# Six of 64 row-maximum reduces of an attention head moved from VectorE to ScalarE and GpSimd

## The reference, cut to what matters

```python
mod = (silu(c) @ wmod).reshape(2, 6, 1, -1)
ga = (2 * (ga >= 0) - 1) * maximum(abs(ga), 0.25)     # a gate, gb likewise
h = layernorm(x) * (1 + ca) + sa
Q, K, V = lora_linear(h, ...)                         # each (2, 2048, 16, 16)
energy = einsum("nqhd,nkhd->nhqk", Q, K) / sqrt(16)
out = einsum("nhqk,nkhd->nqhd", softmax(energy, axis=-1), V)
x = x + ga * lora_linear(out, Wo, bo, Ao, Bo)
h = layernorm(x) * (1 + cb) + sb
x = x + gb * ffn(h)                                   # shared expert + best of 8 experts
```

## Time and profile before

| what | value |
|---|---|
| time, median of 3 runs | 1997.99 us (1996.38 to 2003.76) |
| profiled execution | 2001.02 us, its span 1999.3 us |
| mean granted TensorE clock | 0.978 |
| PE busy | 1883.2 us, 94% |
| VectorE busy | 1576.3 us, 79% |
| ScalarE busy | 1179.2 us, 59% |
| GpSimd busy | 322.2 us, 16% |
| reduces of maxima units | 2048, 1276.8 us busy |

### The profile page before, as it was taken

One profiled execution on the slowest core, in us unless ns is written; L12 is line 12 of the kernel. 1 busy time (PEld: TensorE's weight loads), 2 busy tenths in 40 slices (PEclk: granted clock), 3 DMA queues, 4 the chain that ended last, 5 costly groups with the idle time before them and its releaser, 6 DMA issues.

```text
span 1999.3 us, 33500 instructions
## 1 busy us (share of the span) xinstructions
PE 1883.2 (94%) x12334; PEld 705.1 (35%) x12335; DVE 1576.3 (79%) x2802; ACT 1179.2 (59%) x1354; POOL 322.2 (16%) x361
## 2 busy tenths in 40 slices
PE   7688999999999999999999999999975799999997
PEld 5332222222222222222222222222224555666664
DVE  4377999999999999999999999999816632254443
ACT  4534777777777777777777777777761221111111
POOL 5535000000000000000000000000016532323332
PEclk9898999999999999999999999999997799999999
DMA  4541111211111111111111111111056433222221
GB/s 152 169 148 37 41 41 50 64 44 41 41 60 57 39 41 55 58 46 38 42 60 56 42 38 53 56 43 38 11 171 214 139 106 116 95 78 71 68 66 47
DMA packets 89734, 141.48 MB, mean 71 GB/s; under 512 B 13104, under 2 KB 60208, under 8 KB 89472
## 3 DMA queue, kind: packets, MB, share of 16 engines
q1 hardware_dynamic: 74336, 102.01, 16.2%
q0 software_dynamic: 10240, 32.40, 4.9%
q10 hardware_dynamic: 5024, 5.24, 0.8%
HBM read 90.84 MB, written 48.51 MB: 70 GB/s over the span
## 4 chain that ended last, share of the span: by engine, by line
PE 83%; DVE 4%; issue 4%; POOL 3%; DMA 3%; ACT 1%; SPq 1%; POOLq 0%; DVEq 0%; ACTq 0%
PE ps L853 25%; PE ps L842 21%; PE ps L808 16%; PE ps L1514 7%; PE ps L1065 5%; PE ps L1532 3%; PE ps L1398 3%; DVE mx L909 2%; DMA l_in<-inverse_sums 2%; POOL parts L693 1%; ACT prob L947 1%; POOL rest L689 1%; PE ps L1523 1%; DMA qk_parts<-parts 1%; POOL k_low L681 1%
## 5 line engine op out<-in xcount | busy, mean ns | idle before, releaser
L909 DVE TENSOR_REDUCE mx<-ps 128x1 f32<-128x512 f32 x2048 | 1276.8, 682 | 47.4 <-PE ps L808 42.9
L947 ACT ACTIVATE prob<-ps 128x1024 f32<-128x1024 f32 x1024 | 992.3, 1021 | 294.6 <-PE ps L842 292.3
L853 PE MATMUL ps<-prob,vs 128*32 128x512 f32 x4096 | 546.4, 605 | 0.7 <-ACT prob L947 0.7
L808 PE MATMUL ps<-k_high,q_high 64*128 64x512 bf16 x2048 | 411.9, 388 | 32.4 <-DMA k_low<-qk_parts 17.5
L842 PE MATMUL ps<-q_high,k_high 64*128 64x512 bf16 x2048 | 389.6, 377 | 3.4 <-ACT prob L947 2.5
L842 PE MATMUL ps<-q_low,k_low 34*128 34x512 bf16 x2048 | 389.8, 377 | 0.0
L808 PEld LDWEIGHTS ps<-k_high,q_high 64*128 64x128 bf16 x2048 | 100.9, 92 | 670.6 <-DVE mx L909 603.7
L975 POOL COPY vs<-v_all 128x256 f32 (+1 forms) x32 | 12.7, 400 | 1138.3 <-PE ps L853 1138.2
L842 PEld LDWEIGHTS ps<-q_low,k_low 34*128 34x128 bf16 x2048 | 100.0, 94 | 117.5 <-issue 0.3
L1563 ACT ACTIVATE esig<-ps 128x512 f32<-128x512 f32 x39 | 23.3, 597 | 195.9 <-PE ps L1514 195.9
L842 PEld LDWEIGHTS ps<-q_high,k_high 64*128 64x128 bf16 x2048 | 101.4, 96 | 86.9 <-ACT prob L947 27.9
(11 more groups left out here) (145 smaller groups left out, 1312.4 us busy)
## 6 DMA issues: line engine op xcount, KB each, us to landing
k_high<-qk_parts SPq DMA_DIRECT2D x128, 128.0 KB
qk_parts<-parts SPq DMA_DIRECT2D x32, 384.0 KB, 3.6
q_high<-qk_parts SPq DMA_DIRECT2D x128, 64.0 KB
k_low<-qk_parts SPq DMA_DIRECT2D x128, 64.0 KB
head_out<-head_out_sb SPq DMA_DIRECT2D x32, 256.0 KB, 10.8
sorted_in<-zero_row POOLq DMA_DIRECT2D x13, 390.0 KB, 7.0
xs<-sorted_in SPq DMA_DIRECT2D x39, 130.0 KB
q_low<-qk_parts SPq DMA_DIRECT2D x128, 32.0 KB
```

The costliest lines, as they stand in the source:

```text
L808: pe.matmul(ps[:, ring_bank(2 * m + u), :], q_high[p][mine, t * P:(t + 1) * P], k_high[p][mine, c * CH:(c + 1) * CH], start=True, stop=Tru ...
L853: mm = pe.matmul(ps[32 * j:32 * j + 32, 7, :], vs[buf(h)][:, kt, :], prob[:, kt % 2, j * CH:(j + 1) * CH], start=(kt == 0), stop=(kt == KT ...
L909: dve.tensor_reduce(mx[:, at, c:c + 1], ps[:, ring_bank(k), :], AX.X, ALU.max).then_inc(s_ring, 1)
L947: act.activation(prob[:, kt % 2, :].rearrange("p (u c n) -> p u c n", u=2, c=2)[:, :, half, :], ps[:, 2 * half:2 * half + 2, :], ACT.Exp). ...
```

## The change

**Copied units.** In each head but the first, six pairs (3, 7, 13, 17, 23, 27) have their second unit (u = 1) taken by ScalarE: it copies the bank of 128 x 512 to one of three buffers `taken` behind the exponentials of that iteration, and counts `s_copied`. GpSimd folds the copy to 64 columns in three steps of halving. [...] The six folded units stand in `folded`; one reduce on VectorE turns them into the six columns of `mx`. `mx` and `folded` are doubled.

**Turned maxima.** A table (`Ring`) lists the order of all units and turned maxima, and who frees each bank. The negation is now behind pair 0 of the next head (both units), and the turned maxima behind its third pair (`TURN_AT` = 2).

**Lead.** `LEAD` is 12, so pair 0 falls into iteration 11.

**GpSimd.** The gates are split and stand between the folds of heads 1 and 2; a head's staging and DMA stand behind its second fold. In each head: pair 3, pair 7, staging and DMA, pair 13, 17, 23, 27.

```diff
-LEAD = 10
+LEAD = 12
+TURN_AT = 2
+FOLDS = 3
+FOLDED = 64
+COPIED = (3, 7, 13, 17, 23, 27)
+class Ring:
+    def __init__(self):
+        self.place, self.released = {}, []
+        count = {"dve": 0, "act": 0}
+        for n in range(NH + 1):
+            for m in range(PAIRS if n < NH else 0):
+                for u in range(2):
+                    self.add((n, m, u), "act" if copied(n, m) and u else "dve", count)
+                if n and m == TURN_AT:
+                    self.add((n - 1, "turned"), "dve", count)
+        self.add((NH - 1, "turned"), "dve", count)
...
+        def ring_place(pe, what):
+            at = ring.place[what]
+            if at >= RING:
+                engine, n = ring.released[at - RING]
+                pe.wait_ge(s_ring if engine == "dve" else s_copied, n)
+            return ps[:, ring.bank(what), :]
...
         def max_pair(pe, h, m):
+            banks = [ring_place(pe, (n, m, u)) for u in range(2)]
+            for u in range(2):
...
         def turn_maxima(pe, h):
+            bank = ring_place(pe, (num(h), "turned"))
             pe.wait_ge(s_neg, num(h) + 1)
...
                     if beside:
                         max_pair(pe, who, first)
-                    elif first == 0 and after == 1:
-                        turn_maxima(pe, plus(h, 1))
+                    if first == TURN_AT and num(who) <= NH:
+                        turn_maxima(pe, plus(who, -1))
                     weigh(h, kt - 1)
...
+            def negate(n):
+                if n:
+                    dve.wait_ge(s_fold, n * len(COPIED))
+                    rows = mx[n % 2][:].rearrange("p t c -> p (t c)")[:, UNITS // 2:UNITS // 2 + 30]
+                    dve.tensor_reduce(rows.rearrange("p (i k) -> p i k", k=10)[:, :, 3:8:4], folded[n % 2][:], AX.X,
+                                      ALU.max).then_inc(s_unfold, 1)
+                    dve.wait_ge(s_unfold, n)
+                dve.wait_ge(s_ring, ring.taken((n, PAIRS - 1, 0 if copied(n, PAIRS - 1) else 1)))
+                dve.tensor_reduce(mneg[:], mx[n % 2][:], AX.X, ALU.max, negate=True).then_inc(s_neg, 1)
...
             for n in range(1, NH):
-                head((0, n), last=n == NH - 1)
+                for m in range(PAIRS):
+                    reduce_pair(dve, (0, n), m)
+                    if m == 0:
+                        negate(n - 1)
+                    if m == TURN_AT:
+                        turned_maxima(dve, step, (0, n - 1))
...
+            def take_maxima(n, m):
+                if n >= NH or not copied(n, m):
+                    return
+                k = fold_number(n, m)
+                wait(act, s_fold, k - FOLDS + 1)
+                act.wait_ge(s_max, ring.made((n, m, 1)))
+                act.copy(taken[k % FOLDS][:], ps[:, ring.bank((n, m, 1)), :]).then_inc(s_copied, 1)
...
+            def fold(n, m):
+                k = fold_number(n, m)
+                rows, j = taken[k % FOLDS], COPIED.index(m)
+                pool.wait_ge(s_copied, k + 1)
+                w = CH // 2
+                while w >= FOLDED:
+                    a, b = rows[:, 0:w], rows[:, w:2 * w]
+                    step(pool.tensor_tensor(a, a, b, ALU.subtract))
+                    step(pool.tensor_scalar(a, a, 3.0e38, 0.0, ALU.min, ALU.max))
+                    if w > FOLDED:
+                        step(pool.tensor_tensor(a, a, b, ALU.add))
+                    w //= 2
+                wait(pool, s_unfold, n - 2)
+                pool.tensor_tensor(folded[n % 2][:, j // 2, j % 2, :], a, b, ALU.add).then_inc(s_fold, 1)
...
+            scale_modulation(pool, step)
+            for m in COPIED:
+                fold(1, m)
+                if m == COPIED[1]:
+                    gate(pool, step, 0)
+                if m == COPIED[5]:
+                    gate(pool, step, 3)
+            for n in range(2, NH):
+                for m in COPIED:
+                    fold(n, m)
+                    if n == 2 and m == COPIED[0]:
+                        gate_bias(pool)
+                    if m == COPIED[1] and n + 1 < NH:
+                        following(n)
```

More of the change, by code:

```diff
@@ L112, in close, with add, bank, made @@
         self.count, self.loop = self.first + trips * per, None
+class Ring:
[9 more added lines that the diff above has]
+        self.add((NH - 1, "turned"), "dve", count)
+        self.total = count
+    def add(self, what, engine, count):
+        self.place[what] = len(self.released)
+        count[engine] += 1
+        self.released.append((engine, count[engine]))
+    def bank(self, what):
+        return 4 + self.place[what] % RING
+    def made(self, what):
+        return self.place[what] + 1
+    def taken(self, what):
+        return self.released[self.place[what]][1]
+def copied(n, m):
+    return n > 0 and m in COPIED
+def fold_number(n, m):
+    return (n - 1) * len(COPIED) + COPIED.index(m)
 def buffers(name, shape, dt, region, n=2):
@@ L655, in beside @@
                         for _ in range(share[s]):
-                            reduce_pair(dve, step, (0, 0), next(units))
+                            reduce_pair(dve, (0, 0), next(units))
                 if more2:
@@ L756, in attend_sync, with maxima @@
                 sp.wait_ge(s_parts[o], 16 * (NCH + 1))
-            def maxima(h, last=False):
+            def maxima(h):
                 p = buf(h)
-                sp.wait_ge(s_ring, MAXIMA * (num(h) + 1) + (1 if last else 2))
+                sp.wait_ge(s_ring, ring.taken((num(h), "turned")))
                 for u in range(2):
@@ L778, in turn @@
                 if last >= 1:
-                    maxima(plus(h, 1), last == 1)
+                    maxima(plus(h, 1))
                 if last == 1:
@@ L898, in attend_tensor, with reduce_pair, turned_maxima @@
                 turn((0, n), min(NH - 1 - n, 2))
[L900 to L912 removed]
+        def reduce_pair(dve, h, m):
+            n, t, c = num(h), m // CPB, m % CPB
+            for u in range(1 if copied(n, m) else 2):
+                what = (n, m, u)
+                at = u * HT + t
+                dve.wait_ge(s_max, ring.made(what))
+                dve.tensor_reduce(mx[n % 2][:, at, c:c + 1], ps[:, ring.bank(what), :], AX.X,
+                                  ALU.max).then_inc(s_ring, 1)
+        def turned_maxima(dve, step, h):
+            what = (num(h), "turned")
+            dve.wait_ge(s_max, ring.made(what))
             dve.wait_ge(s_mrows[buf(h)], 64 * (nth(h) + 1))
[L914 removed]
+            turned = ps[0:KT, ring.bank(what), 0:P]
             step(dve.tensor_copy(mb[buf(h)][:, 0, :], turned))
@@ L963, in attend_scalar @@
                         head_copy(n - 1)
+                    before_now = PAIRS * (n + 1) + LEAD + 2 * (kt - 1)
+                    if n or kt:
+                        for ahead in range(2):
+                            take_maxima((before_now + ahead) // PAIRS, (before_now + ahead) % PAIRS)
             head_copy(NH - 1)
```

118 lines of the change are left out of this document (46 added, 72 removed).

## The result

| kernel | time, median (runs) | ratio to before, 95% interval | profiled span | one head |
|---|---|---|---|---|
| before | 1998.4 us (4) | | 1999.3 us | 40.89 us |
| changed | 2047.9 us (2046.5 to 2051.1, 4) | 1.0246 [1.0222, 1.0269] | 2044.0 us | 42.40 us |

The change is slower by 49.5 us. The forecast was 2018.1 us: the sign was right, and the loss is two and a half times the predicted one. The time lies 2 us above the range of 1990 to 2046, and 16 us above the narrower one of 2003 to 2032. Granted clock: 0.978 in both.

What follows compares the result with a forecast made beforehand. It took a chain of PE, the reduce of B0 and the three-bank ring as the bound; change of heads +9, fold waits +10.1 and lead +1 gave +20.1 on 1998.0, so 2018.1 us; own range 2003 to 2032.

Steps and rivals of the forecast that it cites:

- What bounds the kernel: Attention iteration: chain of PE, reduce of B0 (an odd pair's first unit) and three-bank ring, 2.49 us; not VectorE's throughput.
- Copied units: Steady iterations: copying odd pairs' second units idles VectorE 0.60 us six times a head, PE gets nothing; saving 0.
- What would show it: List of expected marks, first: B (odd) pair to next A (even) pair 1.17 us in copied and other iterations alike.
- ScalarE leaks: Rival, exponentials behind copies: 186 copies leak 0.15 us each, 28 us on top, 2046 us; chance 0.10.
- ScalarE: Copies behind the exponentials: 0.59 us each, fitting the 0.55 us spare with next exponentials about 0.1 late; cost 0.
- The change of heads: Between heads: folded reduce and negation delay pair 2, 1.34 us against 1.05; +0.3 us a head, +9 us over 30.
- The folded reduce's length: VectorE's reduce of the folded units at each change of heads: 0.55 us for 384 elements; skill's estimate 0.46.
- GpSimd's fold: Nine dependent operations per copied unit on GpSimd: 5.5 us taken, between estimates of 4.4 and 5.6.
- The waits for the folds: VectorE waiting for GpSimd: 6f - 25.2 (f, one fold's time), +7.8 us first head, +2.3 second; together +10.1.
- The lead: Twelve pairs ahead: +1.85 us before attention, some regained at the end; net +1 us.

Runs made afterwards that it cites:

- e4: e1 without copied units, folds and folded reduce, gates ahead of attention as in the kernel before: 1986.6 us, ratio 0.9938.
- e6: e1 with copies and folds kept, only the folded reduce and its wait for the folds left out: 1985.2 us (one run).
- e1: Changed kernel with one wait per pair, on the later count, where VectorE frees both banks: 2005.7 us, ratio 1.0033.
- e3: Kernel before with a redundant wait ahead of the one there, on the odd pairs alone: 1999.1 us, ratio 0.9997.
- e10: Kernel before with a redundant wait ahead of the one there, on the even pairs alone, without a head's first: 2039.8 us, ratio 1.0207.
- e2: Kernel before with a redundant wait, one count lower, ahead of the one there on every pair but a head's first: 2039.9 us, ratio 1.0203.
- e9: e5 with the ring's waits per unit, each ahead of its own matmul, and the negated-maxima wait back at the transpose: 1982.2 us, ratio 0.9914.
- e5: e4 with the queries wait moved to the pair before and the negated-maxima wait to the third pair's second unit: 1983.8 us, ratio 0.9927.
- e11: Kernel before with the redundant wait of e2 written behind the held wait instead of ahead of it: 1997.6 us, ratio 0.9989.
- e7: e2 with a redundant count five below the held one instead of one below: 2043.9 us (one run).
- e12: e10 with two redundant waits instead of one ahead of the held wait: 2040.2 us, ratio 1.0209.

## Why the prediction was right in sign and wrong in size

The changed kernel splits by ratios of 1998 us: turned maxima and lead -12.4 (e4), copied units 0 (e6), folded reduce and first-head wait +19.0 (e1 - e4), second waits +42.6 (changed - e1). Sum +49.2, measured +49.5.

**What bounds the kernel: right.** The chain PE, reduce of B0, ring, PE adds up in every kernel here, at 2.49 or, with 0.09 more in one link, 2.58. e3 and e10 tested it directly.

**The step that failed: *Copied units*.** It reads "PE gets nothing. Saving: 0", and of the extra wait only "if the extra wait on ScalarE's copy hurt, it would lengthen", without a price, and with 0 taken "since the cycle adds up from its rows". The rows could only vouch for the link of 0.06 with one wait on the pair. The change wrote two waits ahead of every pair, copied or not, the later one the held. That made the link 0.15, a head 42.40 us instead of e1's 41.00, and 31 heads 43 us longer (42.6 by the ratios). It was not in the sum and not in a rival, and in the diff it is one line, the list over `ring_place`.

The price stood in the trace of before. There a head's first pair carries two waits, for the ring and for its queries (the order rows say so), and it comes 1.26 us behind its B pair, where the pairs with one wait need 1.18:

```profile
905.43 0.39 PE L808 MATMUL ps<-k_high,q_high 64*128 64x512 bf16 x2
...
906.69 0.37 PE L808 MATMUL ps<-k_high,q_high 64*128 64x512 bf16 x1
```

Its records show the separate wait passed at 0.039 us and the matmul at 0.145 behind the reduce, as in e2. Once a head, it was hidden in the 1.05 us of the change of heads.

The first mark of "What would show it", B to next A at 1.17 in all iterations, failed at once (1.26), in iterations without copies too; that pointed away from the copies. The rival *ScalarE leaks* ends at 2046 us, next to the measured time, with a wrong cause: its exponentials were not late.

**ScalarE: right.** 0.59 us a copy, 0.586 on average, no leak.

**The change of heads: too dear.** Forecast: 1.34 over two iterations. In e1, whose A pairs carry one wait each but for the head's first:

```profile
871.60 0.39 PE L869 MATMUL ps<-k_high,q_high 64*128 64x512 bf16 x2
...
872.86 0.39 PE L869 MATMUL ps<-k_high,q_high 64*128 64x512 bf16 x2
...
874.18 0.39 PE L869 MATMUL ps<-k_high,q_high 64*128 64x512 bf16 x2
...
875.93 0.39 PE L869 MATMUL ps<-k_high,q_high 64*128 64x512 bf16 x2 [0.49 <-DVE mx L958]
876.52 0.28 PE L875 MATMUL ps<-ident,mneg 128*16 128x128 f32 x1 [0.21 <-DVE mx L958]
876.73 1.07 PE L902 MATMUL ps<-prob,vs 128*32 128x512 f32 x8
...
878.90 0.39 PE L869 MATMUL ps<-k_high,q_high 64*128 64x512 bf16 x2
```

878.90 - 872.86 = 6.04, so 1.06 over 4.98; with the second wait of the first pair, which comes at 872.86 - 871.60 = 1.26 instead of 1.17, it is 1.15. From pair 2 on everything stands where it was put: transpose at +0.59, weighing at +0.80, next A pair at +2.97 (forecast 1.79 + 1.17). What was off is the lateness of pair 2: 1.75 - 1.17 = 0.58 instead of 0.86. The estimate had laid the folded reduce, the negation and B0 end to end with gaps of 0.03. They overlap in part: in the changed kernel the folded reduce starts 0.59 behind the start of the last reduce (0.72 assumed), and B0's 0.14 behind that of the negation (0.25 assumed), 0.24 of the 0.28. In the row of before from which the gap was read, 907.18 to 907.43, the reduce also waited for the negation (`s_neg` in its order row), and the doubled `mx` had taken that wait away. Per head: 0.1 us over before (41.00 to 40.89) instead of 0.3, as a gain of 0.45 and a folded reduce of 0.56.

**The folded reduce's length: right.** 0.54 against 0.55; the lower estimate of 0.46 beside it was too low.

**GpSimd's fold: too dear.** 4.63 against 5.5. The two-input operations had been read well (0.73, 0.46, 0.32 against 0.67, 0.42, 0.30). The min/max ones took 0.40, 0.29 and 0.24 us, where 1.06, 0.62 and 0.40 had been scaled from an operation of 1.94 us on 512 elements, a comparison and a multiplication. The Trainium skill (GPSIMD Engine Reference, Elementwise — side-by-side cycle accounting) gives one-input work about 1 cycle an element, from which the prediction had estimated 0.9 us for the three; they took 0.93. Against it still stand the 1.50 us for 512 elements, and in the same gate of the kernel before a maximum with one constant:

```profile
182.63 1.49 POOL L482 TENSOR_SCALAR gtmp<-gtmp 128x512 f32<-128x512 f32 x1
```

So not each operation with a maximum is cheap. The gate's rows differ from the fold's in arithmetic and in layout (two runs of 256 elements), and no run here separates the two; what sets the price stays open.

**The waits for the folds: too dear.** 1.57 us in the first head (2.83 in e1, whose iterations are shorter) and none in the second, where 7.8 and 2.3 stood. With the fold of 4.63, the forecast's own formula 6f - 25.2 gives 2.6.

**The lead: about right.** e4's -12.4 us, of which the moved turned maxima are 31 x 0.45 = 14.0, leaves +1.6, where +1 was forecast.

Without the second waits the forecast of +20.1 would have met +6.6 (e1). So the sign did not hang on the missing term, but the size was far off either way: two terms of the sum, the change of heads and the waits for the folds, were too dear, and the missing one was larger than the whole sum.

## What to carry to other kernels

Where an engine is held at the same instruction in every iteration, the waits written on that instruction are part of the critical path: have one, or write the one that ends last first, or give each instruction its own. A diff that turns one wait into two in a helper changes the whole loop, so price it like an instruction added: look in the trace for an instruction that already carries two waits, and at the page's number of instructions for what its rows don't show. Relieving a busy engine gives nothing where the bound is a chain through one of its operations: 186 reduces fewer moved no iteration.

The fastest version here is e9 (or e5, from which it can't be told apart), 1982.2 us, 0.9 % below the kernel before. It has the turned maxima behind the third pair, no copied units, one wait on each matmul of maxima. That the changed kernel with its two waits merely swapped would reach e1's time is what e11 leads one to expect; it was not run.

## What the hardware showed that had not been expected

- A second wait on a matmul costs 0.09 us between release and issue if the held wait is written last (link 0.15 for 0.06; e2, e7, e10, e12, the changed kernel, and the first pair of each head in the kernel before), and nothing if it is written first (e11, the transpose of e4) or if the instruction is not held (e3). Two and three waits cost the same.
- All waits but the first written go into one separate instruction: the one in e12 holds two.
- GpSimd's clamp with two constants: 0.40, 0.29 and 0.24 us for 256, 128 and 64 elements; its subtraction and addition of two tensors 0.73, 0.46 and 0.32.
- On VectorE a reduce from SBUF behind one from PSUM starts 0.59 us after the other's start, and one from PSUM 0.14 us after the start of a 0.22 us negation.
